# Last batch's output chain in two halves of two tiles, with dummy matmuls in TensorE's wait, in an attention and expert-choice layer

## The reference

```
h = layernorm(x) * (1 + ca) + sa
query, key = straight part + rotated part, value          # 16 heads of 8
attn = softmax(query @ key.T / 12) @ value
x = x + ga * (attn @ Wo + bo)
h = layernorm(x) * (1 + cb) + sb
S = sigmoid(h @ Wg).T                                     # 8 experts x 2048 tokens
G, I = top_k(S, 512)                                      # each expert takes its 512 best tokens
out = (gelu(h[I] @ W1 + b1) @ W2 + b2) * G
x = x + gb * scatter_add(out at I)
```

## Time and profile before

| | us |
|---|---|
| median of 3 runs | 424.71 (424.31 to 425.78) |
| the profiled execution, its own time | 423.78 |
| its span, first to last instruction | 422.0 |
| mean granted TensorE clock, share of full | 0.881 |
| TensorE matmuls busy | 313.6 (74%) |
| VectorE busy | 270.2 (64%) |
| ScalarE busy | 205.7 (49%) |
| GpSimd busy | 180.6 (43%) |

### The profile page before, as it was taken

How to read it: one execution, slowest core, us unless ns; L and a number is a source line. 1 busy time by engine, 2 the same in 40 slices (tenths; PEclk the granted TensorE clock), 3 DMA queues, 4 the chain that set the end, 5 groups by cost and what they waited for, 6 DMA issues and landing times.

```text
span 422.0 us, 7330 instructions
## 1 busy us (share of the span) xinstructions
PE 313.6 (74%) x2326; PEld 148.7 (35%) x2326; DVE 270.2 (64%) x540; ACT 205.7 (49%) x394; POOL 180.6 (43%) x208
## 2 busy tenths in 40 slices
PE   4998375999999999999989984101378996690930
PEld 3533042323333333333335333100244764460630
DVE  4459878898999999999976934677642442220210
ACT  2654232888888889888886550100033242211200
POOL 5237541666611111111113713000086877788672
PEclk9999679999999999999999998555587999966895
DMA  8322861011111111111002300700023565544332
GB/s 241 86 101 84 299 227 39 7 43 40 40 40 41 40 39 38 39 38 43 26 4 83 97 0 25 206 0 0 2 66 115 121 145 117 112 83 79 28 28 19
DMA packets 34488, 30.39 MB, mean 72 GB/s; under 512 B 5280, under 2 KB 28704, under 8 KB 34464
## 3 DMA queue, kind: packets, MB, share of 16 engines
q1 hardware_dynamic: 28320, 23.65, 18.2%
q0 software_dynamic: 6144, 6.43, 9.1%
HBM read 18.27 MB, written 11.60 MB: 71 GB/s over the span
## 4 chain that ended last, share of the span: by engine, by line
PE 44%; DVE 18%; POOL 16%; issue 10%; DMA 5%; ACT 4%; ACTq 0%; DVEq 0%; SPq 0%; POOLq 0%
PE ps L1225 14%; POOL out L558 10%; PE ps L1188 8%; PE ps L1211 6%; DVE mx L839 5%; POOL ex L547 5%; DVE big L954 3%; PE ps L1426 2%; DMA out<-big,idx 2%; PE ps L1238 2%; ACT osb L667 2%; DVE KB L875 1%; PE ps L1455 1%; DMA k_parts<-big 1%; PE ps L1306 1%
## 5 line engine op out<-in xcount | busy, mean ns | idle before, releaser
L839 DVE TENSOR_REDUCE mx<-ps 128x2 f32<-128x1024 f32 x128 | 148.2, 1218 | 10.0 <-PE ps L1188 10.0
L690 ACT ACTIVATE big<-ps 128x512 f32<-128x512 f32 x256 | 139.3, 598 | 26.5 <-PE ps L1211 24.5
L1225 PE MATMUL ps<-big,VA 128*32 128x256 f32 (+1 forms) x960 | 80.1, 405 | 3.0 <-ACT osb L667 2.3
L1188 PE MATMUL ps<-KB,QB 48*128 48x512 bf16 x256 | 50.6, 397 | 12.1 <-DVE mx L839 10.6
L547 POOL DMA_INDIRECT ex<-rows,idx x32 | 34.3, 1073 | 51.4 <-DVE idx L1058 40.8
L1211 PE MATMUL ps<-QB,KB 51*128 51x512 bf16 x256 | 54.7, 382 | 1.7 <-ACT osb L667 1.1
L558 POOL DMA_INDIRECT out<-big,idx x32 | 50.4, 1574 | 13.1 <-issue 8.8
L736 ACT ACTIVATE big<-ps,b1c 128x512 f32<-128x512 f32 x32 | 22.0, 687 | 66.2 <-PE ps L1426 66.2
L427 POOL TENSOR_TENSOR VA<-Vall,bv_row 128x128 f32 (+1 forms) x16 | 7.3, 454 | 72.2 <-PE ps L1225 72.2
L1426 PE MATMUL ps<-big,w1s 128*128 128x512 f32 x64 | 35.8, 680 | 2.0 <-DVE big L1024 1.6
L1455 PEld LDWEIGHTS ps<-w2s,big 128*128 128x128 f32 x256 | 30.3, 196 | 6.5 <-issue 4.7
(11 more groups left out here) (172 smaller groups left out, 413.9 us busy)
## 6 DMA issues: line engine op xcount, KB each, us to landing
KB<-k_parts SPq DMA_DIRECT2D x32, 96.0 KB
QB<-q_parts SPq DMA_DIRECT2D x32, 96.0 KB
w1s<-in_w SPq DMA_DIRECT2D x8, 256.0 KB, 2.8
w2s<-in_w SPq DMA_DIRECT2D x8, 256.0 KB, 3.0
k_parts<-big SPq DMA_DIRECT2D x4, 384.0 KB, 3.2
q_parts<-big SPq DMA_DIRECT2D x4, 384.0 KB, 4.5
QB<-mxp SPq DMA_DIRECT2D x96, 2.0 KB
rows<-rw SPq DMA_DIRECT2D x1, 1088.0 KB, 6.0
```

The lines of the kernel that those rows point to most:

```text
L690: nc.scalar.activation(PT[:, u, 2 * i + half, kc, :], ps[:, EXP_BANKS[n], :], ACT.Exp, scale=SCALE).then_inc(s_ex, 1)
L839: nc.vector.tensor_reduce(mx[:, u, :].rearrange("p (h a) -> p h a", h=2)[:, :, n], ps[:, max_bank(u, n):max_bank(u, n) + 2, :], AX.X, ALU.max,
L1188: ins = mm(ps[:, max_bank(u, n) + half, :], QB[rows, r, i, qc * 128:(qc + 1) * 128], KB[rows, r, i, :], start=True, stop=True)
L1225: ins = mm(ps[32 * j:32 * j + 32, 6, cols], VA[:, u, kc, j, :], PT[:, u, j, kc, cols], start=kc == 0 and not cols.start, stop=kc == TC - 1 ...
```

## The change

The links of batch 3's chain, from the copy of the last weighting to its gates, are written out in two halves of two tiles (256 columns) each. The halves of one link lie in two PSUM banks: `LAST_O` for the transposed output, `LAST_A` for the two other transposes, `LAST_GATES` for the projection and the gates. Each half has its own count on the semaphores between the engines. The moments' second part (`bn_aggr`), the epsilon and GpSimd's power still take all four tiles at once; GpSimd's program is the same but for the count it waits for, and SP's too. `keep_warm(1)` behind the projection becomes `stay_warm(16)`. The waits of the last out_turn on `s_mxd` go, and one on `s_ex` comes; both counts are complete by then.

```diff
--- before.py
+++ after.py
@@ -36,6 +36,7 @@
 EXP_BANKS = [(4, 5)[n] if n < 2 else (4, 5, 7)[(n + 1) % 3] for n in range(2 * 2 * TC)]
 TURN_BANKS, LAST_TURN = (0, 2), 2
 A_BANKS = (0, 3)
+LAST_O, LAST_A, LAST_GATES = (2, 4), (3, 5), (1, 7)
 CHUNKS, SLOT_BANK = ((0, 2), (2, NE)), (2, 6)
 M_GA, M_SB, M_CB, M_GB = range(4)
 
@@ -337,7 +338,7 @@
                     modrow[:, b:b + 1, M_GB * D:(M_GB + 1) * D].to_broadcast([128, TC, D])).then_inc(w_gb, 16)
 
             for b in range(NB):
-                sp.wait_ge(s_x2, b + 1)
+                sp.wait_ge(s_x2, b + 1 if b + 1 < NB else NB + 1)
                 sp.dma_start(out[b].rearrange("(c p) d -> p c d", p=128),
                              x2[:, b * TC:(b + 1) * TC, :]).then_inc(w_out, 16)
             sp.wait_ge(s_gr, NB)
@@ -512,7 +513,7 @@
                 nc.gpsimd.tensor_tensor(rstd2[:, t4], var2[:, t4], mhalf[:, 0:TC], ALU.pow).then_inc(s_r2, 1)
 
             def rows_2(b):
-                pool.wait_ge(s_xn2, b + 1)
+                pool.wait_ge(s_xn2, b + 1 if b + 1 < NB else NB + 1)
                 rows = rw[:, b * TC:(b + 1) * TC, 0:D]
                 scale, shift = (modrow[:, b:b + 1, m * D:(m + 1) * D].to_broadcast([128, TC, D]) for m in (M_CB, M_SB))
                 nc.gpsimd.tensor_tensor(rows, xn2[:, b % 2], scale, ALU.mult).then_inc(s_xm2, 1)
@@ -702,10 +703,16 @@
                 step(it * 2 + 1, 1)
             step(14, 0)
             step(15, 1, more_max=False, last=True)
-            out_copy(15)
-
-
-            gates_out(3)
+            act.wait_ge(s_pv, NS)
+            act.wait_ge(s_ot, NS - 1)
+            for h in range(2):
+                cols = slice(h * L // 2, (h + 1) * L // 2)
+                nc.scalar.activation(osb[:, cols], ps[:, 6, cols], ACT.Copy).then_inc(s_oe, 1)
+            for h in range(2):
+                cols = slice((3 * TC + 2 * h) * NE, (3 * TC + 2 * h + 2) * NE)
+                act.wait_ge(s_gl, NB + h)
+                ins = nc.scalar.activation(ge[:, cols], ps[:, LAST_GATES[h], cols], ACT.Exp, scale=-1.0)
+            ins.then_inc(s_ge, 1)
 
 
             act.wait_ge(l_top, 16 * 8)
@@ -935,11 +942,52 @@
             gates_in(1)
             normed(14, LAST_TURN)
             gates_in(2)
-            normed(15, LAST_TURN)
-            a_out(3)
-            residual(3)
-            normed_2(3)
-            h2_out(3)
+            for h in range(2):
+                cols = slice(8 * h, 8 * h + 8)
+                dve.wait_ge(s_ot, NS + h)
+                o = ps[:, LAST_O[h], 0:L // 2].rearrange("p (a d) -> p a d", d=32)
+                nc.vector.reciprocal(rs[:, cols].unsqueeze(2), o[:, :, HD:HD + 1]).then_inc(s_rs, 1)
+                dve.wait_ge(s_rs, NS + h)
+                nc.vector.tensor_tensor(
+                    An[:, 3, 2 * h:2 * h + 2, 3, :].rearrange("p q (j d) -> p q j d", d=HD),
+                    o.rearrange("p (q j) d -> p q j d", j=4)[:, :, :, 0:HD],
+                    rs[:, cols].rearrange("p (q j) -> p q j", j=4).unsqueeze(3).to_broadcast([128, 2, 4, HD]),
+                    ALU.mult).then_inc(s_no, 1)
+            dve.wait_ge(s_y, NB - 2)
+            for h in range(2):
+                dve.wait_ge(s_aT, NB + h)
+                nc.vector.tensor_copy(aT[:, 1, h * L // 2:(h + 1) * L // 2],
+                                      ps[:, LAST_A[h], 0:L // 2]).then_inc(s_aTe, 1)
+            for h in range(2):
+                rows = slice(3 * TC + 2 * h, 3 * TC + 2 * h + 2)
+                dve.wait_ge(s_y, NB + h)
+                nc.vector.tensor_tensor(x2[:, rows], ps[:, LAST_GATES[h], 0:2 * D].rearrange("p (c d) -> p c d", c=2),
+                                        X[:, rows, :], ALU.add).then_inc(s_x2, 1)
+                dve.wait_ge(s_x2, NB + h)
+                for n in range(rows.start, rows.stop):
+                    ins = nc.vector.bn_stats(stat2[:, n, :], x2[:, n, :])
+                ins.then_inc(s_st2, 1)
+            dve.wait_ge(s_st2, 2 * NB)
+            for n in range(3 * TC, 4 * TC):
+                ins = nc.vector.bn_aggr(mv2[:, n, :], stat2[:, n, :])
+            ins.then_inc(s_st2, 1)
+            dve.wait_ge(s_st2, 2 * NB + 1)
+            nc.vector.tensor_scalar_add(var2[:, 3 * TC:], mv2[:, 3 * TC:, 1], EPS).then_inc(s_v2, 1)
+            dve.wait_ge(s_r2, NB)
+            dve.wait_ge(s_xm2, NB - 2)
+            dve.wait_ge(s_h2t, NB - 2)
+            for c in range(TC):
+                n = 3 * TC + c
+                ins = nc.vector.tensor_scalar(xn2[:, 1, c, :], x2[:, n, :], mv2[:, n, 0:1], rstd2[:, n:n + 1],
+                                              ALU.subtract, ALU.mult)
+                if c % 2 == 1:
+                    ins.then_inc(s_xn2, 1)
+            dve.wait_ge(s_gl, NB - 2)
+            for h in range(2):
+                cols = slice(h * L // 2, (h + 1) * L // 2)
+                dve.wait_ge(s_h2t, NB + h)
+                nc.vector.tensor_scalar(h2T[:, 1, cols], ps[:, LAST_A[h], 0:L // 2], modcol[:, 3, 3:4], modcol[:, 2, 3:4],
+                                        ALU.mult, ALU.add).then_inc(s_h2e, 1)
             gates_in(3)
 
             dve.wait_ge(l_top, 16 * 8)
@@ -1383,12 +1431,44 @@
                     if n == at:
                         stage(b)
             weigh(15, 1, TC - 1)
-            out_turn(15, LAST_TURN)
-            turn_a(3)
-            project(3)
-            keep_warm(1)
-            turn_h(3)
-            route_gates(3)
+            pe.wait_ge(s_no, NS - 1)
+            pe.wait_ge(s_ex, 16 * NS)
+            for h in range(2):
+                pe.wait_ge(s_oe, NS + h)
+                for c in range(2):
+                    at = (2 * h + c) * 128
+                    ins = nc.tensor.transpose(ps[:, LAST_O[h], c * 128:(c + 1) * 128], osb[:, at:at + 128], ident[:])
+                ins.then_inc(s_ot, 1)
+            pe.wait_ge(s_h2e, NB - 2)
+            for h in range(2):
+                pe.wait_ge(s_no, NS + h)
+                for c in range(2):
+                    ins = nc.tensor.transpose(ps[:, LAST_A[h], c * 128:(c + 1) * 128],
+                                              An[:, 3, 2 * h + c].rearrange("p g d -> p (g d)"), ident[:])
+                ins.then_inc(s_aT, 1)
+            pe.wait_ge(s_x2, NB - 1)
+            pe.wait_ge(s_ge, NB - 1)
+            for h in range(2):
+                pe.wait_ge(s_aTe, NB + h)
+                for c in range(2):
+                    at = (2 * h + c) * 128
+                    ins = mm(ps[:, LAST_GATES[h], c * 128:(c + 1) * 128], aT[:, 1, at:at + 128], wo_g[:, 3, :],
+                             start=True, stop=True)
+                ins.then_inc(s_y, 1)
+            stay_warm(16)
+            for h in range(2):
+                pe.wait_ge(s_xn2, NB + h)
+                for c in range(2):
+                    ins = nc.tensor.transpose(ps[:, LAST_A[h], c * 128:(c + 1) * 128], xn2[:, 1, 2 * h + c, :], ident[:])
+                ins.then_inc(s_h2t, 1)
+            pe.wait_ge(s_x2, NB + 1)
+            for h in range(2):
+                pe.wait_ge(s_h2e, NB + h)
+                for c in range(2 * h, 2 * h + 2):
+                    n = 3 * TC + c
+                    ins = mm(ps[:, LAST_GATES[h], n * NE:(n + 1) * NE], h2T[:, 1, c * 128:(c + 1) * 128], wg[:],
+                             start=True, stop=True)
+                ins.then_inc(s_gl, 1)
             pe.wait_ge(s_g, NB)
             nc.tensor.transpose(ps[:, 3, 0:128], g_en[:].rearrange("p e n -> p (e n)"), ident[:]).then_inc(s_lg, 1)
```

## The result

| | before | changed |
|---|---|---|
| median of 20 runs each, one measurement | 426.52 us (424.31 to 428.25) | 423.59 us (421.78 to 426.26) |
| ratio, 95% interval | | 0.9926 [0.9911, 0.9941] |
| the profiled execution, its own time | 423.78 us | 425.29 us |
| its span | 422.0 us | 423.5 us |
| mean granted TensorE clock | 0.881 | 0.876 |

The kernel is faster by 0.74% by the ratio, or 3.2 us (2.5 to 3.8 by its interval); the two medians differ by 2.9 us. The forecast difference was 3.2 us. The time itself, 423.59 us, lies above the forecast 421.5 us and 0.6 us above its range, because the kernel before takes 426.52 us over 20 runs and not the 424.71 us of the three first ones.

The account below looks back on a forecast made before the run. The bound was a chain of waits from engine to engine, serial in the last batch. Halving its links gains 2.65 to 3.7, taken as 3.2 us: 423.78 to 420.6, plus 0.9 to the median, 421.5 us; range 419.9 to 423.0.

Parts of the forecast that it names:

- the anchor of the time and of its range: Kernel before taken at its shown median, 424.71 us, 0.9 above the profiled execution's; runs differ by about 0.9 us.
- The difference: Last batch's chain gains 2.65 to 3.7 us, taken as 3.2, reaching the end one for one.
- the stretch: From ScalarE's copy of the last weighting to the last gate matmul's end: 9.5 us (9.3 to 10.4) instead of 13.04.
- First part: Copy to osb through the moments, in halves: aggregation starts 1.36 us earlier, with VectorE's queue as the bound.
- Second part: Normalisation through gates, in halves: brings the whole chain's gain to 3.5 us at full clock, 2.65 at low.
- the sum for the low one: Second part at low clock: two transposes about 0.64 us, half the gates 1.04, second half ending at 261.55.
- Dummies: Sixteen on TensorE behind the projection: near 2.0 us, at most 2.44, in idle time, so they cost nothing.
- The middle, 3.2 us: Chain's gain if the clock falls anywhere between the first transposes behind the normalisation and the gates.
- Halves one behind the other: Rival: no half overlaps, each link pays start-up twice, 2.0 us more; 425.5 us, no change; chance 0.07.
- The clock late or never low in the experts: Two rivals: clock returns later, 426.7 us, chance 0.04 (partly, 0.05); clock does not fall at 314, 419.0 us, chance 0.08.

Follow-up runs that it names:

- halves_only: The changed kernel without its sixteen dummies, the one fp32 dummy kept behind the projection: ratio 0.9942 [0.9921, 0.9962], stretch 10.37 us.
- dummies_only: The kernel before with sixteen bf16 dummies in place of the one fp32 dummy, no halves: ratio 0.9999 [0.9973, 1.0026], stretch 13.03 us.
- all_together: Kernel with x added on TensorE and 24 dummies, plus late waits first and the additions of x moved to other waits: ratio 0.9929 [0.9901, 0.9957].
- sum_on_tensor: Changed kernel with x added by TensorE, moments from PSUM, sum copy and scale and shift on ScalarE, 24 dummies: ratio 0.9919 [0.9894, 0.9945].
- followers: The kernel before, whole links, with one small unused instruction added behind four links on ScalarE and VectorE: stretch 13.95 us.
- first_part: The changed kernel with halves only from osb copy to moments, the rest whole, sixteen dummies: ratio 0.9959 [0.9942, 0.9976], stretch 11.67 us.

## Why the prediction was right or wrong

**The step that failed: the anchor of the time and of its range.** The prediction put the kernel before at 424.71 us and allowed "about 0.9 us by which runs differ". Over 20 runs the kernel before is at 426.52 us, with runs from 424.31 to 428.25, and the three first runs lay in the lower part of that. This puts the forecast 1.8 us too low; the measured 423.59 us lie 2.1 us above its middle and 0.6 us above its range. The profiles show where such differences arise: in the fourteen profiled executions ScalarE's last osb copy, which stands ahead of every edit, starts between 250.93 and 254.65 us, and in the two compared above 3.48 us of this come from before the first osb copy, where their low clock differs. That it makes the whole of the spread is not shown. 426.52 less the forecast 3.2 is 423.3 us; 423.59 was measured.

**The difference: right in sum, in part by luck.** 3.2 us were forecast and 3.2 measured (2.5 to 3.8 by the interval); the second measurement of the same two kernels gave 1.6 (0.4 to 2.7). That the halves carry the gain held: halves_only gives most of it, dummies_only none. But the stretch should have been 9.5 us, 10.4 at most, and was 10.69 and 10.43 us in the changed kernel's two profiles; 4.9 us were forecast to the aggregation and 5.22 measured. To the first gather the kernel before took 54.62 and 55.51 us and the changed one 52.53 and 52.25, so the profiles show 2.7 us in the mean. Two things that the prediction did not have stand in this.
- In favour: the kernel before can lose the clock already ahead of the projection, which happened in three of the six executions with whole links ahead of it (2.06 to 2.09 us instead of 1.16), and in none of the eight with halves there. With that the stretch before is 13.95 us instead of 13.04. If it is so half of the time, the mean gain is 0.45 us larger, an estimate from six executions. That the halves protect the clock is not shown. In the three executions the clock fell 3.2 us behind the start of the osb copy, came back, and fell again at 10.0 to 10.1 us. In the other three with whole links the first fall came at 9.0 to 9.5 us, and in the six with halves and VectorE's additions at 8.7 to 9.4, or 12.1 with thirty dummies. So these may have been spared by the moment at which their chain met the clock's changes, halves or not. Of the two kernels with x added on TensorE, all_together had its first fall at 10.0 us and none at 3.2, but TensorE has other work there (in sum_on_tensor it was 10.4).
- Against: from the start of the search to the first gather the changed kernel takes 39.91 us, the one before 39.64, with the same instructions. 0.2 to 0.5 us more stand there in all kernels that have the first part in halves and neither addition of x on TensorE (six of six), 0.2 in followers, none in the others. In the changed kernel it is one wait of VectorE in the search's fourth round, 0.37 us where 0.13 stood before:

```profile
274.19 0.22 DVE L1023 SCALAR_TENSOR_TENSOR big<-big,scale_t 128x4 int32<-128x4 f32 x1 [0.37 <-DVE big L1009]
```

In halves_only it is at the same instruction, in followers one instruction later (0.20 instead of 0.04), in first_part at two places. No run moves it on purpose, and the cause stays open.

**First part.** Forecast 1.36 us earlier, measured 1.03. The term that was mis-sized is the handing over to TensorE, taken as 0.04 and found as 0.14 at three places, with 0.06 more at aT. Turned round it gives 1.29. The copies, additions and moments of a half were right within 0.01 to 0.02, the pair of transposes too (0.42), and half a projection took 0.70 for 0.66.

**Second part.** From normalisation to the last gate 2.92 us were forecast for the full clock and 3.78 for the low one. Measured: 2.93 (thirty dummies) and 3.75 (changed kernel). The agreement is partly luck. With thirty dummies the gates start 0.18 us later than forecast (1.90 instead of 1.72 behind the first normalisation, by the gaps of the wait order among others) and take 1.03 us instead of the 1.20 of the sum. In the changed kernel the transposes ran at the full clock, where the sum for the low one had them slow too.

**Dummies.** They cost nothing, and took 1.91 us for 2.0. That they hold the clock was the wrong part of this step. The prediction read the fall before as coming 3.6 us behind TensorE's last work, and took shorter idle time as help. But the clock fell 8.8 and 9.1 us behind the start of the osb copy with sixteen dummies and 9.2 with one, and 9.0 in the kernel before, with one (its first profile) as with sixteen (dummies_only). "The middle, 3.2 us" rested on a fall between transposes and gates; it came right ahead of the gates in the changed kernel's first profile, and inside them in its second and in halves_only. The ratios do not tell the dummies from one dummy: 0.9926 [0.9911, 0.9941] against 0.9942 [0.9921, 0.9962].

**Rivals.** Halves one behind the other: no, the second addition stands right behind the first half's moments. The Trainium skill (VectorE: DVE Perf Modes, the section on the TRN2 errata) says that many small tiles pay the latency of SBUF each time, and advises 512 elements or more; by that alone the halves should lose. The instructions of VectorE and ScalarE that were halved here read PSUM, some of them with an operand in SBUF beside it. Their rows show a fixed cost too (0.42 for 256 columns against 0.69 for 512), but it falls into time in which the engine waited anyway. The clock late or never low in the experts: the first gather to the end took 116.3 us for 116.2. The clock was low there from 318.0 to 321.4 us, against 314.8 to 321.6 before, so neither late nor gone.

## What to carry to other kernels

In a chain that goes from engine to engine with nothing beside it, two halves in two banks shortened the chain, up to the engine that handles both halves of several links in a row (here VectorE); that engine's own work is then the bound to attack. Of several waits ahead of an instruction write the one that comes late first; in this kernel that took 0.26 us off the first part. Dummy matmuls are worth a run without them: here sixteen had no effect that the runs can tell. Where the clock or the program's start vary from run to run, compare the stretch in the profiles and take the baseline from many runs: three runs of this kernel missed its median by 1.8 us, more than half the effect.

## What the runs showed of the hardware that was not expected

- The order of waits costs time. With the late count waited for last, TensorE starts 0.14 us behind it; with it first, 0.04 us (four places, in both kernels, each way). On VectorE a wait of the same kind stands as DVEq, and costs 0.06 us.
- The granted clock can fall while TensorE has hardly been idle: it fell at 255.8 to 256.4 us in three of the six executions with whole links, between An's transposes and the projection, after a stretch in which TensorE worked some 0.65 us and rested 0.68 to 0.88 us in turn. In the other three the same pattern kept the full clock.
- The granted clock fell with 2.81 us of idle time ahead of the transposes (dummies_only) and was full with 2.93 (halves_only). Sixteen dummies did not move the fall; thirty, which ended 0.52 us ahead of the transposes, moved it by some 3 us.
- VectorE's addition of 128x32 in SBUF took 0.18 us in the eleven executions in which GpSimd had ended or was within 0.14 us of its end, and 0.65 to 0.72 us in the three in which it started in the middle of GpSimd's 128x512 addition. In all three it ended 0.04 to 0.05 us behind GpSimd's.
